# Macaron transformer block on one core: weighing split in two pieces, the attention's input transposed one slot earlier, and a different order at the end of attention

## The reference

```
x = x + 0.5 * ffn(layernorm(x))        # ternary weights with a scale per output
x = x + attention(layernorm(x))        # 16 heads of 8 features, softmax over 256 keys
x = x + 0.5 * ffn(layernorm(x))

ffn(x):  h = silu(x w1') * (x w2')     # 128 -> 512
         h = gelu(h h1');  h = gelu(h h2')   # 512 -> 512, twice
         return h w3'                  # 512 -> 128
```

## Time and profile before

| | |
|---|---|
| median of three runs | 619.1 us (618.34 to 622.76) |
| the profiled execution | 617.05 us |
| its span, first to last instruction | 615.2 us |
| busy: PE, DVE, ACT, POOL | 589.1, 443.6, 466.4, 98.3 us |
| mean granted clock of PE | 0.99 |
| slots 6 and 7 (an even and an odd one) | 292.0 to 305.3 us, 305.3 to 320.8 us |

### The profile page before, as it was taken

The page is one execution under the profiler, slowest core; times in us unless marked ns, Lnnn a source line. Parts: engine busy times, 40 slices in busy tenths (PEclk is TensorE's granted clock), DMA queues, the critical chain, the costliest instruction groups (busy, mean ns, idle before and its releaser), DMA issues.

```text
span 615.2 us, 12580 instructions
## 1 busy us (share of the span) xinstructions
PE 589.1 (96%) x4452; PEld 439.3 (71%) x4452; DVE 443.6 (72%) x1000; ACT 466.4 (76%) x796; POOL 98.3 (16%) x262
## 2 busy tenths in 40 slices
PE   2999999999999999999999999999989999999996
PEld 2788788788686766565656565766678878788785
DVE  7995855868558778798988897885665756855742
ACT  4677977968865578788787878877877977968964
POOL 2092020022021103132231302102020020020000
PEclk9999999999999799999999999999999999999999
DMA  8300000000074306171625343400000001000011
GB/s 282 86 2 1 0 2 1 0 0 1 1 273 145 130 2 220 56 255 62 235 89 187 137 139 142 134 2 1 2 1 1 1 1 36 0 26 8 1 34 37
DMA packets 36693, 42.02 MB, mean 68 GB/s; under 512 B 2464, under 2 KB 27296, under 8 KB 36640
## 3 DMA queue, kind: packets, MB, share of 16 engines
q1 hardware_dynamic: 36640, 41.31, 19.8%
HBM read 22.42 MB, written 18.87 MB: 67 GB/s over the span
## 4 chain that ended last, share of the span: by engine, by line
PE 73%; ACT 9%; DVE 8%; issue 5%; DMA 3%; SPq 1%; POOL 0%; ACTq 0%; DVEq 0%; POOLq 0%
PE bank L1092 39%; PE bank L1204 9%; PE bank L1179 8%; PE bank L1191 4%; PE bank L1193 3%; DVE silu L842 3%; DVE act_lo L833 2%; ACT silu L544 2%; DVE neg_max L883 2%; PE bank L1161 1%; PE bank L1222 1%; PE bank L1169 1%; ACT act_hi L536 1%; ACT act_hi L559 1%; DMA QK<-qk_scratch 1%
## 5 line engine op out<-in xcount | busy, mean ns | idle before, releaser
L1092 PE MATMUL bank<-act_hi,WH 128*128 128x512 f32 x576 | 230.5, 400 | 3.8 <-ACT act_hi L559 1.5
L1092 PE MATMUL bank<-act_lo,WH 128*128 128x512 f32 x576 | 225.7, 392 | 0.0
L883 DVE TENSOR_REDUCE neg_max<-bank 128x2 f32<-128x512 f32 x256 | 166.8, 681 | 32.6 <-PE bank L1179 30.4
L678 ACT ACTIVATE probs<-bank 128x512 f32<-128x512 f32 x256 | 139.3, 598 | 38.6 <-PE bank L1193 37.0
L853 DVE TENSOR_TENSOR act_lo<-full,act_hi 128x512 fp32r<-128x512 f32 x128 | 91.5, 719 | 101.7 <-ACT act_hi L559 101.4
L557 ACT ACTIVATE full<-bank,SG 128x512 f32<-128x512 f32 x128 | 88.1, 688 | 65.8 <-PE bank L1092 65.0
L1092 PEld LDWEIGHTS bank<-act_hi,WH 128*128 128x128 f32 x576 | 108.2, 188 | 31.2 <-ACT act_hi L559 4.7
L1092 PEld LDWEIGHTS bank<-act_lo,WH 128*128 128x128 f32 x576 | 108.3, 188 | 23.1 <-issue 1.0
L1191 PE MATMUL bank<-QK 32*128 32x256 f32 x512 | 96.1, 334 | 0.4 <-ACT probs L678 0.4
L559 ACT ACTIVATE act_hi<-bank,SG 128x512 fp32r<-128x512 f32 x128 | 87.1, 681 | 0.0
L1193 PE MATMUL bank<-m_parts,SEL 32*128 32x256 f32 x512 | 82.1, 280 | 0.0
(11 more groups left out here) (94 smaller groups left out, 570.7 us busy)
## 6 DMA issues: line engine op xcount, KB each, us to landing
qk_scratch<-qk SPq DMA_DIRECT2D x64, 256.0 KB, 2.6
QK<-qk_scratch SPq DMA_DIRECT2D x16, 1024.0 KB, 7.6
raw_rest<-w_ffn SPq DMA_DIRECT2D x4, 512.0 KB, 5.8
out<-X SPq DMA_DIRECT2D x4, 512.0 KB, 3.2
X<-x SPq DMA_DIRECT2D x3, 512.0 KB, 7.7
raw<-w_ffn SPq DMA_DIRECT2D x3, 256.0 KB, 4.5
X<-x SPq DMA_DIRECT2D x2, 256.0 KB, 3.2
WA<-w_att SPq DMA_DIRECT2D x1, 256.0 KB, 5.6
```

What stands on the lines that cost most here:

```text
L678: A.activation(probs[:, v % 8, :], bank[B_BANKS[bb][v]][:, :], ACT.Exp, scale=SCALE)\
L883: D.tensor_reduce(neg_max[:, bb, qt, n0:n0 + 2], bank[(banks or A_BANKS[bb])[u]][:, :].rearrange("p (h k) -> p h k", h=2), axis=AX.X, op=A ...
L1092: ins = MM(dst, a, b, start=k == 0, stop=k == len(todo) - 1)
```

## The change

1. **Weighing in two pieces.** `EARLY_HALF` names for the even slot the steps 1 and 9, for the odd slot 1 and 5. There part kt = 0 is computed two steps earlier than before; part kt = 1 stays.
2. **Even slot.** `tokens_of_o` goes from step 13 to step 9, and with it `norm_o` and `scale_o` on DVE from 14 and 15 to 10 and 11 (`TOKENS`). `project_v` goes from step 9 to 11 and waits for `o_norm` of the same slot. `transpose_att` for pair i + 2 comes into step 13, and waits for the copy of V and for the normalised x, whose last quarter DVE now makes in its step 12 (7, 8, 9, 12 in place of 8, 9, 10, 11).
3. **Odd slot.** Without the transposes, Q goes from step 9 to 7 and K from 11 to 9. `rows_of_max` waits for the copy of the transposed x.
4. **Last batch.** Its scores go round four banks; in its slot and behind it DVE copies `oT` and `onT` in place of ACT; layernorm steps of DVE there move.
5. **Into the second feed-forward stage.** The short slot has six steps; the first tile of `layer1` stands ahead of the last weighing, the second behind it; the steps of batch 15 between the tiles move by one; ACT loads its gelu table right behind the last silu.

```diff
-TOKENS = 13
+TOKENS = (9, 13)
+EARLY_HALF = ((1, 9), (1, 5))
 A_BANKS = ((0, 1, 5) * 5 + (0,), (5, 1, 0) * 5 + (5,))
-B_BANKS = ((2, 3, 7) * 5 + (2,), (7, 3, 2) * 5 + (7,))
+B_BANKS = ((2, 3, 7) * 5 + (2,), (7, 3, 2) * 5 + (7,), (0, 3, 2, 7) * 4)
...
# ACT, layer1
+                    if t == L1_TILES - 1 and table is not None:
+                        load_table(table)
                     if t >= 1:
                         product_hi(n0, t - 1)
...
# ACT, second feed-forward stage
-                    layer1(t1, {0: lambda: evacuate_o(NBATCH - 1), 3: lambda: o_to_sbuf(NBATCH - 1)})
+                    layer1(t1, {0: lambda: evacuate_o(NBATCH - 1), 4: lambda: o_to_sbuf(NBATCH - 1)}, ACT.Gelu)
...
# ACT, attend
-                    if u == (9 if prev else 5) and v_pair is not None:
+                    if u == (11 if prev else 5) and v_pair is not None:
                         set_v(*v_pair)
-                    if u == 7 and ahead is not None:
+                    if u == 13 and bb == 0 and ahead is not None:
                         x_to_sbuf(ahead)
-                    if u in (9, 11) and ahead is not None:
-                        full_part(ahead, (u - 9) // 2)
-                    if u in (10, 12) and ahead is not None:
-                        high_part(ahead, (u - 10) // 2)
+                    if u in (7, 9) and bb == 1 and ahead is not None:
+                        full_part(ahead, (u - 7) // 2)
+                    if u in (8, 10) and bb == 1 and ahead is not None:
+                        high_part(ahead, (u - 8) // 2)
...
# DVE, attend
+                    if u == 3 and not more:
+                        o_to_sbuf(b - 2)
                     if u == 6 and prev2:
                         add_att(b - 2, 2 * b - 4)
+                    if u == 7 and not more:
+                        evacuate_o(b - 1)
                     if u in side:
                         side[u]()
-                    if u == TOKENS + 1 and prev:
+                    if u == TOKENS[bb] + 1 and prev:
                         norm_o(b - 1)
-                    if u == TOKENS + 2 and prev:
+                    if u == TOKENS[bb] + 2 and prev:
                         scale_o(b - 1)
...
                     even = {u: lambda t=t: normalise(n, tile0 + t, t, 1, last=t == 3)
-                            for t, u in enumerate((8, 9, 10, 11))}
+                            for t, u in enumerate((7, 8, 9, 12))}
...
-                    odd = dict(zip((4, 5, 7, 8, 9, 11), norm_steps(norm_of(q), 4 * q, 4, halves=True)))
+                    odd = dict(zip((4, 7, 8, 9, 10, 11), norm_steps(norm_of(q), 4 * q, 4, halves=True)))
...
# DVE, behind the last slot
             low_x(NB, 0, 1)
+            o_to_sbuf(NBATCH - 2)
             low_x(NB + 1, 1, 5)
...
# PE, attend
-                        if v >= 7 and v % 4 == 3:
+                        if v >= 5 and v % 4 == 1 and u in EARLY_HALF[bb]:
                             weigh(*at, v // 4 - 1, 0)
+                        if v == UNITS and not own:
+
+                            pe.wait_ge(exp_done, UNITS * NBATCH - 1 + CREDIT)
+                            layer1(NB * HT, NB, general, tiles=range(1))
+                            weigh(*at, GROUPS - 1, 0)
+                            weigh(*at, GROUPS - 1, 1)
+                            layer1(NB * HT, NB, general, tiles=range(1, 2))
+                        elif v >= 7 and v % 4 == 3:
+                            if u - 2 not in EARLY_HALF[bb]:
+                                weigh(*at, v // 4 - 1, 0)
                             weigh(*at, v // 4 - 1, 1)
...
+                    if u == 7 and bb == 1 and ahead is not None:
                         if prev2:
                             pe.wait_ge(att_added, b - 1)
                         pe.wait_ge(m_lo, b + 1)
+                        project_q(ahead, 6)
+                    if u == 9 and bb == 1 and ahead is not None:
+                        pe.wait_ge(q_full, ahead)
+                        project_k(ahead, 6)
+                    if u == TOKENS[bb] and own and prev:
+
+                        if bb == 1 and ahead is not None:
+                            pe.wait_ge(k_full, ahead)
+                        else:
+                            pe.wait_ge(att_added, b - 1)
+                        tokens_of_o(b - 1)
+                    if u == (11 if prev else 5) and v_pair is not None:
+
+                        if prev:
+                            pe.wait_ge(o_norm, b)
+                        pe.wait_ge(m_lo, b + 1)
                         project_v(v_pair, 6)
-                    if u == 7 and ahead is not None:
...
+                    if u == 13 and bb == 0 and ahead is not None:
                         pe.wait_ge(v_set, pair + 2)
                         transpose_att(ahead, 0, 6)
```

More of the change, by code:

```diff
@@ L536, in product_hi, with layer1 @@
                 A.activation(act_hi[0][:, t // HT, t % HT, :], silu[:, t % SLOTS, :], ACT.Copy).then_inc(h_hi, 1)
-            def layer1(n0, between={}):
+            def layer1(n0, between={}, table=None):
                 for t in range(L1_TILES):
@@ L608, in body @@
                         last_product()
-                        load_table(ACT.Gelu)
+                        if f == 0:
+                            load_table(ACT.Gelu)
                         side = {}
@@ L692, in o_to_sbuf, with attend @@
                 A.activation(onT[:, :], bank[6][:, 0:SEQ], ACT.Copy).then_inc(on_T_sb, 1)
-            def attend(b, bb, prev=True, prev2=True, own=True, steps=UNITS, ahead=None, v_pair=None):
+            def attend(b, bb, prev=True, prev2=True, own=True, more=True, steps=UNITS, ahead=None, v_pair=None):
                 for u in range(steps):
@@ L699, in attend @@
                         if v < UNITS:
-                            exp_unit(b - d, (bb + d) % 2, v)
-                        if v == UNITS + 3 and own:
+                            exp_unit(b - d, 2 if not more and d == (not own) else (bb + d) % 2, v)
+                        if v == UNITS + 3 and own and more:
                             evacuate_o(b - d)
@@ L719, in att_body @@
             def att_body(i, par, ahead=True, more=True, first=False):
-                attend(2 * i, 0, prev=not first, prev2=not first, v_pair=(i + 1, 1 - par) if more else None)
-                attend(2 * i + 1, 1, prev2=not first, ahead=i + 2 if ahead else None)
+                attend(2 * i, 0, prev=not first, prev2=not first, v_pair=(i + 1, 1 - par) if more else None,
+                       ahead=i + 2 if ahead else None)
+                attend(2 * i + 1, 1, prev2=not first, more=more, ahead=i + 2 if ahead else None)
             att_body(0, 0, first=True)
@@ L729, in _ @@
             att_body(NPAIR - 1, 1, ahead=False, more=False)
-            attend(NBATCH, 0, own=False, steps=SKEW + 4)
+            attend(NBATCH, 0, own=False, more=False, steps=SKEW + 2)
             ffn_phase(1)
@@ L1029, in _, with o_to_sbuf, evacuate_o @@
             ffn_phase(0)
+            def o_to_sbuf(b):
+                dve.wait_ge(on_T, b + 1)
+                D.tensor_copy(onT[:, :], bank[6][:, 0:SEQ]).then_inc(on_T_sb, 1)
+            def evacuate_o(b):
+                dve.wait_ge(pv_mm, GROUPS * b + GROUPS + CREDIT)
+                D.tensor_copy(oT[:, :, :].rearrange("p r t -> p (r t)"), bank[4][:, :]).then_inc(o_out, 1)
             def attend(b, bb, prev=True, prev2=True, more=True, side={}):
@@ L1096, in w_of, with layer1 @@
                 return WH[:, c, P * t:P * t + P], WL[:, c, P * t:P * t + P]
-            def layer1(n0, nblk, general, between={}):
-                for t in range(L1_TILES):
+            def layer1(n0, nblk, general, between={}, tiles=range(L1_TILES)):
+                for t in tiles:
                     j, n = t // HT, n0 + t
@@ L1187, in scores @@
                 rows = slice(32 * lane, 32 * lane + 32)
-                wait(pe, exp_done, UNITS * b + v - used_last(B_BANKS[bb], B_BANKS[1 - bb], v) + 1 + CREDIT)
+                mine = B_BANKS[2 if b == NBATCH - 1 else bb]
+                wait(pe, exp_done, UNITS * b + v - used_last(mine, B_BANKS[1 - bb], v) + 1 + CREDIT)
                 for i in range(2):
-                    dst = bank[B_BANKS[bb][v]][:, SEQ * i:SEQ * i + SEQ]
+                    dst = bank[mine[v]][:, SEQ * i:SEQ * i + SEQ]
                     MM(dst, k_of(2 * par + bb)[rows, 2 * jj + i, P * kt:P * kt + P],
@@ L1324, in ffn_bodies @@
                     pe.wait_ge(xlo_done, NB + 2)
-                    layer1(t1, nb, general, {1: tokens, 3: lambda: transpose_o(b), 4: lambda: project_out(b)})
+                    pe.wait_ge(o_out, NBATCH)
+                    layer1(t1, nb, general, {2: tokens, 4: lambda: transpose_o(b), 5: lambda: project_out(b)},
+                           range(2, L1_TILES))
                     pe.wait_ge(att_added, NBATCH)
@@ L1340, in attend @@
             def attend(b, pair, par, bb, prev=True, prev2=True, own=True, more=True, steps=UNITS,
```

(12 more changed lines are left out.)

28 lines of the change are left out of this document (7 added, 21 removed).

## The result

The changed kernel takes 639.95 us in the median (636.8 to 642.89, five runs) against 619.1 (615.51 to 622.76, five runs): ratio 1.0332, interval 1.0271 to 1.0393. It is slower, as forecast, but by 20.9 us and not by 9.8, and outside the range. The profiled execution took 640.67 us, its span is 638.8; against the span before that is +23.6.

A forecast was written before the change was run, and what follows sets the result against it. TensorE's own work and waits bound the kernel. Five slot pairs +10.5, pair 6 +1.5, slots 13 and 14 +0.4, last batch -1.1, second stage -0.3, gelu table -1.16: +9.8 on 619.1, predicted 629 us, range 615 to 636.

The forecast's parts named there:

- The two waits of the even slot: Even slot: TensorE waits 1.15 us for `scale_o` ahead of V's projection and 0.88 us for DVE's last quarter of x.
- An undisturbed even slot: Even slot in pairs 1 to 5: 1.15 and 0.88 of waits, 0.58 of transposes, 0.1 for pieces, +2.7 us.
- `transpose_o` would stand 3.2 to 3.3 us into its slot: Sign in the even slot's timeline: `transpose_o` comes 3.2 to 3.3 us after its slot's start, as before.
- the gelu wait: Second feed-forward stage: with gelu's table loaded behind the last silu, PE's wait of 1.52 us falls to 0.4, gaining 1.16.
- DVE is in time: Rival, chance 0.13: `scale_o` and x's last quarter are done when PE asks, early half frees 0.39; -8.6 us, 610.5.
- only one wait is real: Rival, chance 0.12: only one of the even slot's two waits occurs; without that for x, 624.5 us.
- the odd slot's -0.6: Odd slot: transposes gone -0.58, wait for K +0.2, pairs ahead of weighings -0.3, boundary +0.1; -0.6 us each, five pairs.
- the wait for K: Odd slot: K needs bank 6 back from ACT's copy of Q, a new wait of 0.2 us.
- the wait for X: Odd slot: the 0.33 us idle for `add_att`, behind DVE's maximum of step 6, stays, with Q now in that place.
- pauses take away waits in the pairs: Even slot: piece boundaries (0.14) and step 1's 0.1 stand against pair waits the new pauses remove; taken as +0.1 us.
- slot 12: Even slot of pair 6, which projects V but transposes nothing: 1.15 us of wait and boundaries, +1.5 us.
- The clock, a rival at 0.10: Rival, chance 0.10: even-slot pauses make TensorE's clock fall; one or two falls give 634 to 638 us, five pairs 652.

## Why the forecast fell short

**Right: direction and the bulk.** The two waits of the even slot were forecast at 1.15 and 0.88 and measured 1.09 and 0.86. The chain from the pair to `o_nat` was 2.36 both times. An undisturbed even slot grew by 2.84 (slot 8), forecast 2.7. That `transpose_o` would stand 3.2 to 3.3 us into its slot was right too (339.22 less 335.98 is 3.24), and so was the gelu wait, 0.3 in place of 0.4. The rivals "DVE is in time" and "only one wait is real" are refuted by these rows, and by what the run with `norm_o` ahead gave back.

**Wrong: the odd slot's -0.6.** That is the step that failed. It gave -3.0 over five slots and the trace shows +1.1, a miss of 4.1, in two terms. The first is the pieces in the odd slot, which the forecast took at -0.3 and +0.1 (and that of step 1 at nothing). Inside the change the pieces cost 0.4 in an odd slot (the run without them), a miss of 0.6 in each of five; in the kernel before, alone, they cost 0.1. The second stood in no sum: I counted what the move takes from TensorE (0.58 of transposes) and what it asks of ACT (the wait for K, 0.2: measured 0.17 in slot 7), but did not follow GpSimd's queue, which the subtractions behind Q and K are on, nor ask what DVE, whose `var` had moved too, does at that moment. Slots 3, 5 and 7 each hold a meeting, at about 0.9 us; 2.7 in all. Against both stands that the move itself gave more than forecast: without the pieces and without a meeting the slots 3 and 7 are 0.8 to 0.9 shorter than before and slot 11 is 0.4, where 0.58 less 0.2 was in the sum; the wait for X, which the forecast kept, is gone there.

**Wrong in size: the pieces in the even slot and in slot 12.** I costed them at +0.1 in the even slot, "pauses take away waits in the pairs". Alone they cost 0.6 there. Within the change it shows little, because the moved V waits for DVE anyhow: without the pieces the even slot is only 0.3 shorter (15.93 for 16.21). In slot 12 (+2.4 for +1.5) it shows in full: without the pieces 14.79 for 15.54. Slots 13 and 14 are 0.4 and 0.6 shorter without them too; by which wait slot 14 grew 0.7 I haven't found.

**The clock, a rival at 0.10, came in small.** It fell twice, in slots 6 and 10, for 3.4 us each, which made them 17.7 in place of 16.2: 1.53 us a fall, 3.1 in all. In slot 6 it fell at 316.40, right behind the second of the two pauses, which ended at 316.29. I had priced one or two falls at 5 to 9 us, after the long stretch of the first slot. All three kernels in which TensorE stands idle 1.0 to 1.1 us ahead of V show such a fall in an even slot (two in the changed kernel, one each in the runs with the layernorm steps early and without the pieces); none of the other ten profiles does, not even that of the run with `norm_o` ahead, which keeps five pauses of 0.86. So the long pause goes with it, but five or six of them give one or two falls, and I can't say which. Elsewhere the clock fell in other kernels too (10.2 us from slot 15 on with the pieces alone, 3.4 us in the second feed-forward stage of two runs), for which I have no cause. The Trainium skill, "TensorE: Matmul & The Clock Gate", section "A second HAM failure mode: psum-queue depth-cycling", speaks of a clock that swings between its two levels through frequent short idle spells; here it fell in two of the five slots that have pauses of 1.09 and 0.86 us, and in none of those with 0.3 alone.

**Not the change, or not shown to be.** In the profiled execution 2.3 us were gone before the attention began, in code that was not touched; in the other kernels that start lies anywhere from 204.4 to 207.4. In slots 0 and 1 the clock was low from 210.5 to 224.2, 13.7 us, and before for 10.2; other profiles have 3.4 to 27 us there. A forecast made on one execution can't see this. Slot 1, which the forecast took at 0, also holds a meeting: it takes 15.00, and 14.05 with the layernorm steps early.

**The whole, by the medians.** Of the 20.9 us, 2.6 are clock. At equal clock the change costs 18.3 us; of that the pieces make 7.6 (the run without them stands at 624.3), the moves about 13, and the end gives back 2.3. Alone, in the kernel before, the pieces cost 6.0.

**The end.** Slot 15 gained 0.7 of 1.1, the second stage 1.2 of 1.5. What came back there: `project_out` of batch 15 waits 1.5 for ACT's copy of `onT`, and the wait for `x_lo` is 2.6 and was 1.5.

## What to carry to other kernels

When work is moved, follow everything that hangs on it, on every engine, to the place where it lands: what stood in no sum here was a subtraction on GpSimd that appears in none of TensorE's waits, and it cost because it landed on a VectorE instruction that row maxima stand behind. A block put earlier to fill a wait pays only if the wait's own chain is shortened with it, and splitting it has a price. And before a consumer is placed behind an engine's result, write down that engine's list between the two: the two even-slot waits could be read off it to 0.06 us.

## What the runs showed of the hardware

- **GpSimd can hold up even a tiny VectorE instruction.** A `TENSOR_SCALAR` of 128x4 elements took 1.29 us in place of 0.16 beside a `TENSOR_TENSOR` of 128x512 on GpSimd that had started 0.04 us before (slot 7), and 0.16 with the same 0.04 in slot 9, where GpSimd's took 1.35; a subtraction 0.06 us after DVE's end (the kernel before) costs nothing. So less than the records resolve decides over 0.9 us of a slot, and neighbouring slots of the same code fall on either side. Row maxima out of PSUM that began under the same subtractions kept their 0.68 to 0.69.
- **A short fall of the clock**, 3.4 us at a granted clock of 0.51, cost 1.53 us of a slot that was bound by TensorE for most of it; over whole runs a microsecond at the lower level costs about 0.38, by the estimate above.
- **The pieces of a weighing** (8 records) take 0.57 us from start to next start where a whole one (16) takes 1.00.
